# The first unit of a cross-attention and mixture-of-experts kernel: low parts and masks in another order, first keys and first queries on banks of their own

## The reference

```
q = layernorm(x) @ Wq.T + bq          # 16 heads of 8
k, v = ctx @ Wk.T + bk, ctx @ Wv.T + bv
scores = where(mask == 0, -inf, q @ k.T / sqrt(8))     # one 512x154 mask for all
x = x + softmax(scores) @ v @ Wo.T + bo
xf = layernorm(x);  logits = xf @ Wg;  top 2 of 16 experts
y = sum over the two experts of gate * ((silu(xf@W1+b1) * (xf@W11+b11)) @ W2 + b2)
z = (silu(xf@Ws1+bs1) * (xf@Ws11+bs11)) @ Ws2 + bs2    # shared expert
x = x + y + z
```

## Time and profile before

| what | value |
|---|---|
| median of 3 runs | 307.57 us (305.07 to 308.53) |
| profiled execution, its own time | 307.24 us |
| its span | 305.4 us |
| mean granted TensorE clock | 0.976 of full speed |
| TensorE matmuls busy | 273.2 us, 89% of the span |
| VectorE busy | 205.6 us, 67% |
| ScalarE busy | 149.5 us, 49% |
| GpSimd busy | 142.4 us, 47% |
| start of the turned scores of unit 0 (L1177) | 23.36 us from the start of the span |

### The profile page before, as it was taken

The page is one execution under the profiler, slowest core; times in us unless marked ns, Lnnn a source line. Parts: engine busy times, 40 slices in busy tenths (PEclk is TensorE's granted clock), DMA queues, the critical chain, the costliest instruction groups (busy, mean ns, idle before and its releaser), DMA issues.

```text
span 305.4 us, 6071 instructions
## 1 busy us (share of the span) xinstructions
PE 273.2 (89%) x1836; PEld 206.2 (68%) x1836; DVE 205.6 (67%) x723; ACT 149.5 (49%) x313; POOL 142.4 (47%) x229
## 2 busy tenths in 40 slices
PE   7777899999998999989998999999689999999920
PEld 7654456656556555655564567888589999999920
DVE  2767646665668678765797468782357787886864
ACT  2414687657573655655554744322234644554400
POOL 3546433724433126844338403756006666766660
PEclk9799999999999999999999999999999999999975
DMA  6999940667892000000001100118714968868176
GB/s 211 377 367 397 406 167 3 67 71 95 250 393 95 0 3 0 27 28 17 2 0 36 38 1 2 52 35 240 231 36 129 291 206 260 281 203 262 48 254 206
DMA packets 28495, 44.22 MB, mean 145 GB/s; under 512 B 2752, under 2 KB 16192, under 8 KB 28464
## 3 DMA queue, kind: packets, MB, share of 16 engines
q1 hardware_dynamic: 21808, 36.52, 35.8%
q0 software_dynamic: 6656, 7.31, 10.8%
HBM read 27.00 MB, written 14.73 MB: 137 GB/s over the span
## 4 chain that ended last, share of the span: by engine, by line
PE 62%; DVE 16%; DMA 10%; issue 5%; POOL 5%; ACT 2%; DVEq 0%; POOLq 0%; ACTq 0%; SPq 0%
DVE mpad L563 6%; PE ps L1191 5%; PE ps L1415 5%; PE ps L1421 5%; PE ps L1149 5%; PE ps L1432 5%; PE ps L1177 5%; DMA result_rows<-yo,dest 4%; PE ps L1187 4%; PE ps L1150 4%; PE ps L1175 4%; POOL slot_rows L841 3%; PE ps L1162 3%; PE ps L1099 2%; PE ps L1205 2%
## 5 line engine op out<-in xcount | busy, mean ns | idle before, releaser
L563 DVE TENSOR_REDUCE mpad<-ps 128x2 f32<-128x312 f32 x128 | 55.6, 476 | 36.3 <-PE ps L1150 36.0
L913 POOL DMA_INDIRECT result_rows<-yo,dest x47 | 45.1, 960 | 39.5 <-DVE yo L765 37.4
L791 POOL TENSOR_SCALAR ks<-k_stack,cst 128x160 fp32r<-128x160 f32 x64 | 30.1, 482 | 70.3 <-DVE k_stack L548 70.2
L978 ACT ACTIVATE pf<-ps 128x512 f32<-128x512 f32 x80 | 46.5, 596 | 15.4 <-PE ps L1191 10.9
L1150 PE MATMUL ps<-ks,qs 96*128 96x312 f32 x128 | 45.5, 411 | 0.0
L1149 PE MATMUL ps<-mq_b,identb 128*128 128x312 bf16 x128 | 38.3, 305 | 4.9 <-DVE mpad L563 2.4
L841 POOL DMA_INDIRECT slot_rows<-xr,slot x32 | 31.4, 983 | 14.2 <-issue 13.9
L1177 PE MATMUL ps<-qs,ks 128*128 128x512 f32 x64 | 37.2, 583 | 0.0
L1149 PEld LDWEIGHTS ps<-mq_b,identb 128*128 128x128 bf16 x128 | 12.3, 96 | 32.7 <-issue 26.9
L1086 ACT ACTIVATE e_s<-ps,wu 128x128 f32<-128x128 f32 x62 | 19.4, 363 | 22.0 <-PE ps L1415 22.0
L1432 PE MATMUL ps<-wd,e_h 128*128 (+1 forms) x188 | 29.0, 277 | 1.1 <-DVE yo L765 1.1
(11 more groups left out here) (184 smaller groups left out, 605.1 us busy)
## 6 DMA issues: line engine op xcount, KB each, us to landing
wu<-w_biased SPq DMA_DIRECT2D x31, 322.0 KB, 4.4
wr<-w_up SPq DMA_DIRECT2D x1, 5152.0 KB, 25.1
w_biased<-wr SPq DMA_DIRECT2D x1, 5152.0 KB, 16.8
slot_rows<-zero SPq DMA_DIRECT2D x1, 3120.0 KB, 27.4
xg<-slot_rows SPq DMA_DIRECT2D x12, 260.0 KB, 3.4
wd<-w_down SPq DMA_DIRECT2D x1, 2048.0 KB, 11.9
xo<-result_rows SPq DMA_DIRECT2D x3, 512.0 KB, 5.1
xs<-bor POOLq DMA_DIRECT2D x1, 1024.0 KB, 11.3
```

What stands on the lines that cost most here:

```text
L563: dve.tensor_reduce(mpad[:, m % 2, q, 96 + 2 * a:98 + 2 * a], ps[:, KS_ + a, 0:2 * SKM].rearrange("p (c k) -> p c k", c=2), AX.X, ALU.max, ...
L913: pool.indirect_dma_start(out=result_dram[:, :], out_offset=bass.IndirectOffsetOnAxis(ap=dest[:, n:n + 1], axis=0), in_=yo[:, n % 4, :], i ...
L978: act.activation(pf[:, n % RP, :], ps[:, ST_ + n % 2, :], ACT.Exp, scale=DK ** -0.5).then_inc(exp_done, 1)
```

## The change

All of it lies in the first unit, but for one wait in `score_rows`, which every unit runs.

- **Banks:** the first keys (b = 0, m = 0) go to `M_` in place of `Q_`. The first queries go in two halves of 256 tokens, the first to `Q_`, the second to `O_`. So they need not wait until `k_stack` has read the keys.
- **TensorE:** 22 filler calls in place of 14 at the start; the 3 behind the keys go, and the 6 behind the queries become 4. `first_queries` makes high-high and low-high products of both halves behind `x_hi`, and only the last product of each half waits for `x_lo`. `score_rows` waits for two `ks` before each of its calls (for all four before the first until now), and the two first calls of `score_rows` don't wait for the whole `qs`; the very first waits for its first half. `values(0, 0)` stands before the third `score_rows`, and `queries(0, 1)` behind it.
- **VectorE:** `mpad` is cleared in pieces, with its constant column set at the start; `wk_lo` stands before the normalization; `c_lo` is made here, behind `wq_lo` (it was GpSimd's); the masks are parted into `row_mask` (behind `k_stack`) and `column_mask` (behind the row maxima); `qs` of m = 0 is made in two halves; `value_rows` moves ahead of the third row maximum, `q_stack(0, 1)` behind the last.
- **ScalarE:** the high parts of `wv` and `wg` stand behind the first `k_part`; `q_part` in two halves; the masked columns of `mpad`, two copies of 128x104, are made here from `mq_b` (they were VectorE's).
- **GpSimd:** `context_low(0)` goes.

```
--- before.py
+++ after.py
@@ -225,6 +225,10 @@
...
         AB_, SUM_ = 2, (0, 6)
 
+        def key_bank(b, m):
+
+            return M_ if b == 0 and m == 0 else Q_
+
         TX_, A_, B_, Y_ = 0, 2, 4, 6
 
...
@@ -505,34 +509,42 @@
...
                                   x_hi[:, c * S:(c + 1) * S].bitcast(F32), ALU.subtract).then_inc(xlo_done, 1)
 
-            dve.memset(mpad[:, :, :, :], 0.0)
+            low = 96 + HG
+            dve.memset(mpad[:, :, :, 0:low], 0.0)
+            for i in range(2):
+                dve.memset(mpad[:, i, :, low + SK - P:low + SK - P + 1], MASKED)
+            dve.memset(mpad[:, :, :, low + SK - P + 1:P], 0.0)
             for v, first in ((cum, 0), (nb, 1), (thr, P)):
                 dve.memset(v[:, 0, :], float(first))
+            dve.memset(mq_b[:, :, SK:SKM], MASKED / 2)
+
+            def low_weights(count, hi, lo, raw):
+
+                dve.wait_ge(whi_done, count)
+                dve.tensor_tensor(lo[:, :], raw[:, :], hi[:, :].bitcast(F32), ALU.subtract).then_inc(wk_split, 1)
+
             dve.wait_ge(ld_x, 16)
             block_statistics(0).then_inc(ln_var, 1)
+            low_weights(1, wk_hi, wk_lo, wk_raw)
             norm_block(0)
-            for count, (hi, lo, raw) in enumerate(((wk_hi, wk_lo, wk_raw), (wq_hi, wq_lo, wq_raw))):
-                dve.wait_ge(whi_done, count + 1)
-                dve.tensor_tensor(lo[:, :], raw[:, :], hi[:, :].bitcast(F32), ALU.subtract).then_inc(wk_split, 1)
+            low_weights(2, wq_hi, wq_lo, wq_raw)
+            dve.wait_ge(ctx_hi_done, 1)
+            dve.tensor_tensor(c_lo[:, :], ctx_s[:, 0, :], c_hi[:, :].bitcast(F32), ALU.subtract).then_inc(ctx_split, 1)
             dve.wait_ge(ld_c, 32)
             dve.tensor_scalar(mbk[:, :], vec[:, V_BK:V_BK + NG], cst[:, C_MK:C_MK + 1], None, ALU.mult)
             dve.tensor_scalar(mbq[:, :], vec[:, V_BQ:V_BQ + NG], cst[:, C_MQ:C_MQ + 1], None,
                               ALU.mult).then_inc(bias_done, 1)
-            dve.tensor_copy(identb[:, :], ident)
             low_block(0)
 
-            def masks():
-
+            def row_mask():
+
+                dve.tensor_copy(identb[:, :], ident)
                 dve.wait_ge(ld_m, 32)
-                dve.memset(mq_b[:, :, SK:SKM], MASKED / 2)
-                for dst, src in ((mq_b[:, :, 0:SK], mq_raw[:, :, :]), (mk_b[:, :], mk_raw[:, :])):
-                    last = dve.tensor_scalar(dst, src, 0.0, MASKED, ALU.is_equal, ALU.mult)
-                last.then_inc(consts_done, 1)
-                low = 96 + HG
-                for i in range(2):
-                    dve.memset(mpad[:, i, :, low + SK - P:low + SK - P + 1], MASKED)
-                    dve.tensor_scalar(mpad[:, i, :, low:low + SK - P], mq_raw[:, :, P:SK], 0.0, MASKED, ALU.is_equal,
-                                      ALU.mult)
+                dve.tensor_scalar(mq_b[:, :, 0:SK], mq_raw[:, :, :], 0.0, MASKED, ALU.is_equal, ALU.mult).then_inc(consts_done, 1)
+
+            def column_mask():
+
+                dve.tensor_scalar(mk_b[:, :], mk_raw[:, :], 0.0, MASKED, ALU.is_equal, ALU.mult).then_inc(consts_done, 1)
 
             def other_lows():
...
@@ -545,7 +557,7 @@
...
                 reach(dve, k_part_done, b, 4, m + 1)
                 reach(dve, ks_done, b, 16, 4 * m - 4)
-                dve.scalar_tensor_tensor(out=k_stack[:, m % 2, :], in0=ps[:, Q_, 0:SKP],
+                dve.scalar_tensor_tensor(out=k_stack[:, m % 2, :], in0=ps[:, key_bank(b, m), 0:SKP],
                                          scalar=vec[:, V_BK + m % 4:V_BK + m % 4 + 1], in1=k_part[:, m % 2, :].bitcast(F32),
                                          op0=ALU.add, op1=ALU.subtract).then_inc(k_stack_done, 1)
...
@@ -555,6 +567,18 @@
...
                                          scalar=vec[:, V_BQ + m % 4:V_BQ + m % 4 + 1], in1=q_part[:, m % 2, :].bitcast(F32),
                                          op0=ALU.add, op1=ALU.subtract).then_inc(qs_done, 1)
+
+            def first_queries():
+
+                for i in range(2):
+                    cols = slice(S // 2 * i, S // 2 * i + S // 2)
+                    if i:
+                        dve.wait_ge(q_part_done, 1)
+                    else:
+                        dve.wait_ge(q_half, 1)
+                    last = dve.scalar_tensor_tensor(out=qs[:, 0, cols], in0=ps[:, (Q_, O_)[i], cols], scalar=vec[:, V_BQ:V_BQ + 1],
+                                                    in1=q_part[:, 0, cols].bitcast(F32), op0=ALU.add, op1=ALU.subtract)
+                    last.then_inc((qs_half, qs_done)[i], 1)
 
             def row_max(b, m, q):
...
@@ -658,16 +682,17 @@
...
 
             key_stack(0, 0)
-            masks()
+            row_mask()
+            first_queries()
             other_lows()
-            q_stack(0, 0)
             row_max(0, 0, 0)
             key_stack(0, 1)
             row_max(0, 0, 1)
+            value_rows(0, 0)
             row_max(0, 0, 2)
+            row_max(0, 0, 3)
+            column_mask()
             q_stack(0, 1)
-            row_max(0, 0, 3)
-            value_rows(0, 0)
             row_max(0, 1, 0)
             for b in range(B):
...
@@ -894,7 +919,6 @@
...
             pool.memset(vx[:, :, DK:DK + 1], 1.0)
             pool.tensor_copy(vl[:, :, :, DK:DK + 1], cst[:, C_QUAD:C_QUAD + HG].unsqueeze(1).unsqueeze(3).to_broadcast([P, NG, HG, 1])).then_inc(cleared, 1)
-            context_low(0)
             key_stacks(0, 0)
             key_stacks(0, 1)
...
@@ -956,7 +980,7 @@
...
                 reach(act, k_mm, b, 4, m + 1)
                 reach(act, k_stack_done, b, 4, m - 1)
-                act.activation(k_part[:, m % 2, :], ps[:, Q_, 0:SKP], ACT.Identity, bias=mbk[:, m % 4:m % 4 + 1],
+                act.activation(k_part[:, m % 2, :], ps[:, key_bank(b, m), 0:SKP], ACT.Identity, bias=mbk[:, m % 4:m % 4 + 1],
                                scale=cst[:, C_MK:C_MK + 1]).then_inc(k_part_done, 1)
 
...
@@ -1032,14 +1056,30 @@
...
                         copy_rows(b, -1)
 
+            def first_queries():
+
+                for i in range(2):
+                    act.wait_ge((q_first, q_mm)[i], 1)
+                    cols = slice(S // 2 * i, S // 2 * i + S // 2)
+                    act.activation(q_part[:, 0, cols], ps[:, (Q_, O_)[i], cols], ACT.Identity, bias=mbq[:, 0:1],
+                                   scale=cst[:, C_MQ:C_MQ + 1]).then_inc((q_half, q_part_done)[i], 1)
+
+            def mask_rows():
+
+                act.wait_ge(consts_done, 1)
+                low = 96 + HG
+                for i in range(2):
+                    act.activation(mpad[:, i, :, low:low + SK - P], mq_b[:, :, P:SK], ACT.Copy).then_inc(mpad_done, 1)
+
             context_high(0, 0)
+            high_block(0)
+            act.wait_ge(bias_done, 1)
+            k_hi(0, 0)
             act.wait_ge(ld_w, 48)
             for hi, raw in ((wv_hi[:, :], wv_raw), (wg_hl[:, 0:NE], wg_s)):
                 act.activation(hi, raw[:, :], ACT.Copy).then_inc(whi_done, 1)
-            high_block(0)
-            act.wait_ge(bias_done, 1)
-            k_hi(0, 0)
-            q_hi(0, 0)
+            first_queries()
+            mask_rows()
             k_hi(0, 1)
             q_hi(0, 1)
...
@@ -1114,14 +1154,14 @@
...
 
             pe.wait_ge(pool_cleared, 1)
-            keep_clock(14)
+            keep_clock(22)
             pe.wait_ge(ld_c, 32)
 
...
                 reach(pe, qs_done, b, 4, m)
                 w = slice(P * (m % 4), P * (m % 4) + P)
-                split_mm(ps[:, Q_, 0:SKP], wk_hi[:, w], wk_lo[:, w], c_hi[:, 0:SKP], c_lo[:, 0:SKP]).then_inc(k_mm, 1)
+                split_mm(ps[:, key_bank(b, m), 0:SKP], wk_hi[:, w], wk_lo[:, w], c_hi[:, 0:SKP], c_lo[:, 0:SKP]).then_inc(k_mm, 1)
 
             def queries(b, m):
...
@@ -1140,9 +1180,10 @@
...
             def score_rows(b, m, q):
 
-                reach(pe, qs_done, b, 4, m + 1)
-                reach(pe, ks_done, b, 16, 4 * m + 4)
+                if b or m or q >= 2:
+                    reach(pe, qs_done, b, 4, m + 1)
                 for a in range(2):
+                    reach(pe, ks_done, b, 16, 4 * m + 2 * a + 2)
                     reach(pe, max_done, b, 32, 8 * m + 2 * q + a - 1)
                     o = ps[:, KS_ + a, 0:2 * SKM].rearrange("p (c k) -> p c k", c=2)
...
@@ -1305,24 +1346,38 @@
...
                         logits(b, -1)
 
+            def first_queries():
+
+                pe.wait_ge(xhi_done, 1)
+                pe.wait_ge(wk_split, 2)
+                w = slice(0, P)
+                halves = ((Q_, slice(0, S // 2)), (O_, slice(S // 2, S)))
+                for bank, cols in halves:
+                    pe.matmul(ps[:, bank, cols], wq_hi[:, w], x_hi[:, cols], start=True, stop=False)
+                    pe.matmul(ps[:, bank, cols], wq_lo[:, w], x_hi[:, cols], start=False, stop=False)
+                pe.wait_ge(xlo_done, 1)
+                for (bank, cols), done in zip(halves, (q_first, q_mm)):
```

(19 more changed lines are left out.)

## The result

The changed kernel took 305.18 us (median of 4, 304.97 to 305.54), the kernel before 308.05 in the same comparison (305.07 to 310.21). The ratio is 0.990, 95% interval 0.9863 to 0.9937. Forecast: 304.9, range 303.0 to 307.5. The profiled executions took 304.97 and 307.24, a difference of 2.27 where 2.5 was forecast.

What follows compares the result with a forecast made beforehand. TensorE was taken to bound 24 to 100 us, so only the start of unit 0's turned scores counts: 2.6 us earlier, less 0.1 for ports, gives 304.7 from the profiled execution or 305.1 from the median; forecast 304.9, range 303.0 to 307.5.

Steps and rivals of the forecast that it cites:

- The front: First unit, up to its turned scores (measured from the landing of `x`): start at 20.76 for 23.36, 2.6 us gained.
- Which step limits: First score rows: `ks` on GpSimd is late next, four ready at 14.25 us (now 15.05), behind the halved queries.
- `c_lo` and the normalization: VectorE at the start: without GpSimd's `c_lo` beside it, the 898 ns normalization takes about 0.34 us, 0.56 us gained.
- `wk_lo` beside `rstd`: VectorE's wait for `rstd` before the normalization: `wk_lo` fits there, costing 0 to 0.1 us, at worst 0.6.
- The order at the end: End of the first unit's row maxima: `q_stack` (0.66 us) and `v_all` (0.34 us) leave the path.
- The extra wait: `score_rows`, 62 more waits on TensorE's queue: at most 0.045 us each, taken as 0.
- rival D: `score_rows`: the added wait holds second products, 0.045 to 0.09 us in each of 62 calls, giving 309.2 us; chance 0.06.
- The sum: Whole kernel: 2.6 us gained in the first unit, less 0.1 for ports, is 2.5 us; forecast 304.9 us.
- The clock: TensorE in the first unit: 22 filler calls keep it full from 7.6 us, without the half clock of 11 to 14.4.

Runs made afterwards that it cites:

- context_back: The changed kernel with `c_lo` made on GpSimd again, everything else as changed; median 306.07 us, ratio 0.9935 to the kernel before.
- wait_alone: The kernel before with one edit, `score_rows` waiting for two `ks` ahead of each of its calls; median 307.60 us, ratio 0.9986 to the kernel before.
- filler_alone: The kernel before with one edit, 22 filler calls at the start in place of 14; median 306.90 us, ratio 0.9982 to the kernel before.
- lows_alone: The kernel before with `wk_lo` ahead of the normalization, `wq_lo` and `c_lo` behind it on VectorE; median 306.91 us, ratio 0.9964 to the kernel before.
- lows_few_filler: The kernel before with the low parts in the new order and 2 filler calls behind the queries for 6; 312.00 us, ratio 1.0158.

## Why the prediction was right, point by point

- **The front** was forecast at 2.6 less 0.1, and came at 2.44 counted from the landing of `x`. Reductions were to end at 15.28 and 19.30 and ended at 15.31 (14.83+0.48) and 19.30; turned scores 20.76, came 20.70. As `x` landed 0.21 early, each step behind the keys was really 0.2 later than my sums. It is all in the keys: they start 0.09 late, and from their start to `k_part` it is 0.64 us (10.33 to 10.97) where I put 0.49. `ks` took 2.30 as I had it. That the end came out at 20.70 all the same is luck of the landing.
- **Which step limits.** That `ks` would be late next was right. `qs` is whole at 13.36 and the second call starts at 14.34, behind `ks`, so of the cheaper queries about 1 us goes unused, and the halves, whose worth I never asked for, bring nothing that shows.
- **`c_lo` and the normalization**: 0.56 forecast, 0.47 to 0.55 measured, both ways. **`wk_lo` beside `rstd`**: nothing, as the sum had it. The rule of the Trainium skill (SBUF — State Buffer, "Who interferes with whom") held for `c_lo` beside the normalization (0.90 us for 0.34, ending 0.08 behind `c_lo`) and not for `rstd`, which reads 4 columns: 1.04 and 0.69 us, undisturbed, with `rstd` first. By the printed starts the held normalization was even 0.02 ahead of `c_lo` (8.57 and 8.59), still overlapping the one before it; in context_back `c_lo` was ahead (8.28 and 8.35).
- **The order at the end**: I counted 1.0 for it, the run gives 0.6 to 0.85.
- **The extra wait** is the step that failed. "I take 0, as the second stretch, which is where the new wait stands, has no loss with the wait it has" was read from a unit in which nothing had held the first call. It costs 0.62 us in the changed kernel and 0.70 in wait_alone, by the copies of the maxima. The mechanism was rival D's. Its sign, second products 0.05 or more longer, came in 19 of 60 calls by their starts, at the 0.09 that D names, but what remains of it is 0.62/62 = 0.010 us a call, a quarter of the point from which it would have decided.
- **The sum** came out right with help: 2.66 of lead (0.21 by luck), 0.6 lost to the wait, 0.9 won in one wait for transfers, which varies from profile to profile, 0.7 given back at the end. Without the last two the 2.27 would be 2.0, and with `x` landing as before 1.8.
- **The clock** stayed full in the changed kernel as forecast, though it rose at 5.3 and not at 7.6, but my account of the filler was incomplete. In the kernel before, the filler behind the queries runs at half clock until 15.72, 0.1 ahead of `qs` (15.84). An earlier `qs` ends there: it took what filler_alone won and a part of what lows_alone won.
- **The median moved 0.4 more than the forecast.** That is no more than noise: the ratio's interval means anything from 1.9 to 4.2 us. Where the spread comes from can be read. In the first comparison the 17 executions of the kernel before that its ratio uses go from 305.12 us at a granted clock of 0.981 to 309.67 at 0.968, correlation -0.86. 0.013 of the clock over 307 us is 8 us more at half clock. A fall of 3.41 us cost 1.24 and 1.33 in the traces (context_back, lows_few_filler), so 8 us make about 3 of the 4.5 us, an estimate. The changed kernel's four lie within 0.6 us at 0.982 and 0.983, but its variants with 22 calls spread too, down to 0.971 (context_back). Whether any edit steadies the clock is not settled.

## What to carry to other kernels

When the steady state is bound by one engine, count only the moment at which its stream starts, and undo each edit alone: here only one of the parts that were undone showed by itself, and a gain made early was taken by the next engine's order (`wv` and `wg` ahead of `x_hi`), by the filler, or by `ks`. A wait that is always fulfilled is not free in a loop that runs 64 times: it cost 0.09 us in the calls that a row maximum had just held. And filler that keeps the clock up is work ahead of what follows it; taking some away gained nothing, and in the one trace of it the clock fell at a much dearer place.

## What the runs showed of the hardware

- The granted clock is printed as 1.00 in the first microseconds, while the zero products are paced as at half clock (changed kernel: 15 in the 3 us from 2 to 5, 24 in 2.62 us from 6 on). The moment of the first rise differs from run to run: 5.3 us in the changed kernel, 7.6 before, 5.2 to 8.0 in the others, always behind zero products that had run since 1.75.
- A fall of 3.41 us in the second unit cost 1.24 and 1.33 us of lead (context_back, lows_few_filler). What one in the first unit costs no run isolates; two profiles of one kernel with the fall at 12.0 and at 11.2 differ by 0.36 in the front. What brings a fall is open: TensorE was busy for 1.53 of 3.5 us ahead of the fall at 23.8, and in the kernel before for 1.49 us of the same stretch, and there no fall came.
- A GpSimd instruction with two inputs of 288 columns held a VectorE instruction of 0.34 us until it had ended (0.90 and 0.89 in the kernel before and wait_alone, 0.82 in context_back and filler_alone); one of 4 columns did not lengthen the VectorE instruction beside it (0.69), though it lasts 1.04 us. The two pairs differ in their operations as well, so that the columns decide is not shown.
- One more fulfilled wait ahead of a matmul delayed the matmul by 0.09 us in 19 calls, each with a row maximum that had ended 0.15 to 0.17 us before, and not at all in 41 (changed kernel and wait_alone alike).
